# A hybrid attention and state-space kernel: q and k turned once, their parts laid out by DMA, values weighed head by head

## What is computed

```
qkv = x @ qkv_w + qkv_b                      # x: normed, [512, 128]
q, k, v = split(qkv)                         # 16 heads of 8
q, k = rotary(q), rotary(k)
weights = softmax(q k^T * SCALE)             # 512 x 512 per head
x = x + (weights @ v) @ out_w + out_b
```

## Time and profile before

| what | value |
|---|---|
| median of the runs shown | 10320.33 us |
| the profiled execution, its own time | 10330.53 us |
| its span, first to last instruction | 10328.1 us |
| PE, DVE, ACT, POOL busy | 90%, 86%, 70%, 59% |
| mean granted clock of TensorE | 0.986 |
| one sample to the next (load of x to load of x) | 642.4 us |
| attention, first row maximum to the addition at L1371, 16 samples | 72.3 to 75.1 us, mean 73.9 |
| end of L1626 to the next sample's first row maximum, 15 times | 60.5 to 62.3 us, mean 61.4 |

### The profile page before, as it was taken

One profiled execution on the slowest core, in us unless ns is written; L12 is line 12 of the kernel. 1 busy time (PEld: TensorE's weight loads), 2 busy tenths in 40 slices (PEclk: granted clock), 3 DMA queues, 4 the chain that ended last, 5 costly groups with the idle time before them and its releaser, 6 DMA issues.

```text
span 10328.1 us, 259854 instructions
## 1 busy us (share of the span) xinstructions
PE 9306.5 (90%) x88874; PEld 6451.6 (62%) x88874; DVE 8861.6 (86%) x16781; ACT 7278.4 (70%) x15068; POOL 6118.0 (59%) x4900
## 2 busy tenths in 40 slices
PE   7989899898998989989899899999898999899988
PEld 4656656566565665656656566565665656656566
DVE  6978979789797887979879798797987979879798
ACT  5867768677686776857768576685766858668586
POOL 2936829367293772927729277392763928639286
PEclk9999999999999999999999999999999999999999
DMA  0000000000000000000000000000000000000000
GB/s 21 0 3 1 2 3 0 3 1 2 3 0 3 1 2 3 0 3 1 2 3 0 3 1 2 3 0 3 1 2 3 0 3 1 2 3 0 3 1 3
DMA packets 648478, 23.66 MB, mean 2 GB/s; under 512 B 629185, under 2 KB 647250, under 8 KB 647506
## 3 DMA queue, kind: packets, MB, share of 16 engines
q1 hardware_dynamic: 647890, 16.11, 3.7%
HBM read 9.40 MB, written 4.19 MB: 1 GB/s over the span
## 4 chain that ended last, share of the span: by engine, by line
DVE 27%; PE 23%; issue 18%; POOL 17%; ACT 11%; DVEq 1%; POOLq 1%; DMA 0%; SPq 0%; ACTq 0%
POOL work L1700 16%; DVE work L1601 10%; DVE work L1591 6%; ACT scan_in L1099 4%; PE ps L605 4%; PE ps L595 3%; PE ps L590 3%; PE ps L534 2%; PE ps L522 2%; ACT da L983 1%; DVE stats L1223 1%; ACT yscT L1132 1%; DVE scan_in L1505 1%; POOL skip_u L1673 1%; PE ps L801 1%
## 5 line engine op out<-in xcount | busy, mean ns | idle before, releaser
L1700 POOL TENSOR_TENSOR work<-work,crep 128x512 f32<-128x512 f32 x4608 | 5764.0, 1276 | 4134.8 <-DVE work L1540 3631.6
L1099 ACT ACTIVATE scan_in<-du,bcn 128x256 f32<-128x256 f32 x8832 | 3690.6, 498 | 70.5 <-PE ps L811 37.7
L1601 DVE TENSOR_TENSOR_SCAN work<-da,hend,ps 128x256 f32<-128x256 f32 x4608 | 3028.5, 726 | 56.9 <-PE ps L811 47.8
L811 PE MATMUL ps<-w_ident,scan_in 128*128 128x128 f32 x18432 | 2456.3, 278 | 275.9 <-ACT scan_in L1099 147.0
L811 PEld LDWEIGHTS ps<-w_ident,scan_in 128*128 128x128 f32 x18432 | 2019.6, 142 | 873.8 <-DVE work L1601 313.3
L1591 DVE TENSOR_TENSOR_SCAN work<-da,ps 128x512 f32<-128x512 f32 x2048 | 2353.4, 1201 | 38.8
L801 PE MATMUL ps<-work,w_sel 128*32 128x256 f32 x17792 | 1408.6, 390 | 275.4 <-POOL work L1700 274.7
L1017 ACT ACTIVATE work<-ps,w_gate_b 128x512 f32<-128x512 f32 x512 | 351.7, 687 | 870.9 <-PE ps L590 802.8
L801 PEld LDWEIGHTS ps<-work,w_sel 128*32 128x32 f32 x17792 | 376.1, 108 | 755.0 <-POOL work L1700 538.1
L1330 DVE TENSOR_REDUCE smax<-ps 128x1 f32<-128x512 f32 x1024 | 657.7, 685 | 176.4 <-PE ps L499 172.3
L983 ACT ACTIVATE da<-ps 128x512 f32<-128x512 f32 x1024 | 555.8, 605 | 152.3 <-PE ps L522 144.8
(11 more groups left out here) (204 smaller groups left out, 12458.2 us busy)
## 6 DMA issues: line engine op xcount, KB each, us to landing
hend<-work SPq DMA_DIRECT2D x2304, 1.0 KB, 1.8
x_in<-in_x SPq DMA_DIRECT2D x17, 256.0 KB, 2.8
out<-work SPq DMA_DIRECT2D x16, 256.0 KB
gate_w<-in_gate_w SPq DMA_DIRECT2D x1, 1024.0 KB, 5.0
up_w<-in_up_w SPq DMA_DIRECT2D x1, 1024.0 KB, 7.1
down_w<-in_down_w SPq DMA_DIRECT2D x1, 1024.0 KB, 9.1
w_w_zy<-in_w_zy SPq DMA_DIRECT2D x1, 256.0 KB
work<-in_w_mix SPq DMA_DIRECT2D x1, 256.0 KB
```

Source lines behind the costliest of these rows:

```text
L811: mm = eng.transpose(ps[:, bank, c:c + P], scan_in[:, m, tb, 2 * j + s].rearrange("p k c -> p (k c)"), ident[:])
L1099: ins = eng.activation(scan_in[:, m, tb, :, k, :], du[:, hf, tb, :].rearrange("p (e c) -> p e c", c=GC), ACT.Copy, scale=bcn[:, hf, tb, 0, ...
L1601: ins = eng.tensor_tensor_scan(hst[:, p % NHID, half], da[:, 1, 2 * p + s, :], ps[:, RING[p % 4], half], hend[:, 2 * p + s:2 * p + s + 1], ...
L1700: eng.tensor_tensor(prod[:, to, :].rearrange("p (s t) -> p s t", s=2), hst[:, p % NHID, :].rearrange("p (s t) -> p s t", s=2), crep[:, hf, ...
```

## The change

q and k of all heads are turned to feature-major once, by eight fp32 transposes after the rotation (`start`, step 3 on PE). ScalarE and VectorE split the turned array into three parts of [128, 2, 512]. SyncE stores the parts to DRAM (3 DMAs) and loads them from there into the rows of `heads`: 18 DMAs of eight partitions by eight heads by 512, and two for the constant rows, for each half of the heads (`load_heads`). Semaphores `heads_in[0]` and `heads_in[1]` guard heads 0 to 7 and 8 to 15. `turn_head`, `copy_head` and the slot copies are gone.

The norm of the next x moves from the second mixture to the end of the last scan unit, the qkv products to the mixture's beginning. `weigh` takes one head at a time, one key block in each quarter of the array, in two halves of 256 queries at b = 2 and 3 of every iteration; three heads share a bank, and `turn_out` (now a product with a 32-column selector) also sums the four quarters. Rescores rotate through two banks. Every `copy_max` is on ScalarE. There are six outputs to normalise instead of four. Before the loop the preparation of sample 0 runs alone, as before.

```diff
-HG = 4
+HG = 3
+HR = 4
-RESCORE = (3, 4, 6)
+RESCORE = (3, 4)
+QKV_BANK = (6, 2)
-PE_START, ACT_START = (1, 2, 3), (4, 7)
-DVE_START = ((1,), (2,), (3,), (4, 5), (6,), (7,), (8,), (9,))
+PE_ROT = 2
+ACT_START = (9, 11)
+DVE_START = ((5,), (6,), (), (7,), (8,), (0, 2), (), (9,))
+WEIGH_AT = (2, 3)
...
+            def load_heads(at, step=0):
+
+                for n in range(PARTS):
+                    if n < PARTS - 1:
+                        eng.wait_ge(part_a.sem, part_a.count(at, n + 1))
+                    else:
+                        eng.wait_ge(part_v.sem, part_v.count(at, 1))
+                    eng.dma_start(parts_d[n].rearrange("k p t -> p k t"), parts[:, n]
+                                  ).then_inc(parts_kept.sem, parts_kept.up(at))
+                eng.wait_ge(parts_kept.sem, parts_kept.last(at))
+                for g in range(HALVES):
+                    rows = slice(g * HH * HD, (g + 1) * HH * HD)
+                    for k in range(2):
+                        for q in range(SLOTS):
+                            n = q % PARTS if k else q // PARTS
+                            eng.dma_start(
+                                heads[HD * q:HD * (q + 1), g * HH:(g + 1) * HH, k, :],
+                                parts_d[n, k, rows].rearrange("(h c) t -> c h t", c=HD)
+                                ).then_inc(heads_in[g].sem, heads_in[g].up(at))
+                    for k, rows in enumerate((BIAS - QR, BIAS + 2 - QR)):
+                        eng.dma_start(
+                            heads[QR:QR + rows, g * HH:(g + 1) * HH, k, :],
+                            pad_d[k, 0:rows].rearrange("r (o t) -> r o t", o=1).broadcast_to([rows, HH, T])
+                            ).then_inc(heads_in[g].sem, heads_in[g].up(at))
...
                 def score(h, qb):
-                    if qb == 0:
-                        eng.wait_ge(qk_copied.sem, qk_copied.count(at, h + 1))
+                    if qb == 0 and h % HH == 0:
+                        eng.wait_ge(heads_in[h // HH].sem, heads_in[h // HH].count(at, 2 * SLOTS + 2))
...
+                def weigh(h, part):
+
+                    eng.wait_ge(exped.sem, exped.count(at, TB * (h + 1)))
...
+                    q = slice(part * TH, (part + 1) * TH)
+                    for kb in range(TB):
+                        mm = eng.matmul(ps[32 * kb:32 * kb + 32, 7, q],
+                                        vaug[:, kb, h, :], probsT[:, h % HR, kb, q],
+                                        start=(h % HG == 0 and part == 0),
+                                        stop=((h % HG == HG - 1 or h == NH - 1) and part == 1))
...
-                keep_busy(4, 0)
-                turn_head(0)
-                keep_busy(20, 0)
-                turn_head(1)
...
+                weigh(NH - 1, 0)
+                weigh(NH - 1, 1)
+                turn_out(OUTS - 2)
+                turn_out(OUTS - 1)
...
             def mixture(at, coming=None):
-                keep_busy(24, 1)
+                if coming is None:
+                    keep_busy(24, 1)
+                else:
+                    start(coming, 1)
+                    eng.wait_ge(x3_ready.sem, x3_ready.count(at, 1))
+                    start(coming, 2)
+                    keep_busy(4, 1)
...
+                if coming is not None:
+                    eng.wait_ge(qkv_taken.sem, qkv_taken.count(coming, 2))
                 for u in range(4):
                     into(u)
```

More of the change, by code:

```diff
@@ L386, in begin_with @@
             seen = [list(s.seen) for _, s in sems]
-            for step in range(steps):
+            for step in steps:
                 start(Place(0, 0), step)
@@ L530, in weigh @@
                         eng.wait_ge(v_ready.sem, v_ready.count(at, 1))
[L531 to L537 removed]
+                    if h > 0 and h % HG == 0:
+                        eng.wait_ge(o_copied.sem, o_copied.count(at, h // HG))
@@ L627, in mixture @@
                         into(2 * e + 5)
-                    if coming is not None and e in PE_START:
-                        start(coming, PE_START.index(e))
+                    if coming is not None and e == PE_ROT:
+                        eng.wait_ge(summed.sem, summed.count(at, 1))
+                        start(coming, 3)
             def ssm_inputs(at):
@@ L911, in _ @@
             eng.wait_ge(fold_kept, 2)
-            begin_with(start, len(PE_START))
+            begin_with(start, range(4))
             with eng.Fori(0, B) as b:
@@ L1028, in mixture @@
                     if coming is not None and u in ACT_START:
-                        start(coming, ACT_START.index(u))
-                if coming is not None:
-                    for step in range(len(ACT_START), 2 + PARTS):
-                        start(coming, step)
+                        start(coming, 2 + ACT_START.index(u))
             def ssm_inputs(at):
@@ L1184, in _ @@
             eng.wait_ge(prepared, 1)
-            begin_with(start, 2 + PARTS)
+            begin_with(start, range(4))
             with eng.Fori(0, B) as b:
@@ L1206, in _ @@
                 back_v(at, 1, 1)
+                start(Place(b + 1, 0), 1)
                 back_last(at, 1, 1)
@@ L1279, in start @@
                               for n in ("cosine", "sine")]
-                    for half, (first, second, op) in enumerate(((even, odd, ALU.subtract), (odd, even, ALU.add))):
-                        eng.tensor_tensor(ta, first, angles[0], ALU.mult)
-                        eng.tensor_tensor(tc, second, angles[1], ALU.mult
-                            ).then_inc(nchain.sem, nchain.up(at))
+                    first, second, op = ((even, odd, ALU.subtract), (odd, even, ALU.add))[half]
+                    if half == 1:
@@ L1284, in start @@
                         eng.wait_ge(nchain.sem, nchain.last(at))
-                        ins = eng.tensor_tensor(r[:, half], ta, tc, op)
-                        if half == 0:
-                            ins.then_inc(nchain.sem, nchain.up(at))
-                            eng.wait_ge(nchain.sem, nchain.last(at))
-                    ins.then_inc(rot_done.sem, rot_done.up(at))
-                first = [qk_slots[:, :, :, PARTS * n, :] for n in range(PARTS)]
-                full = rot.rearrange("p b (k h c) -> p k b h c", k=2, c=HD)
@@ L1375, in mixture @@
                 norm(at, n_moe, x_res)
+                if coming is not None:
+                    start(coming, 3)
+                    start(coming, 4)
                 eng.wait_ge(routed.sem, routed.count(at, 1))
@@ L1452, in mixture @@
                 eng.wait_ge(vchain.sem, vchain.last(at))
-                if coming is not None:
-                    start(coming, 0)
                 for e in range(NE):
@@ L1646, in _, with begin @@
             eng.wait_ge(prepared, 1)
-            begin_with(start, 10)
+            def begin(at, step):
+                if step < 2:
+                    start_norm(at, step)
+                if step != 1:
+                    start(at, step)
+            begin_with(begin, range(10))
             with eng.Fori(0, B) as b:
```

256 lines of the change are left out of this document (122 added, 134 removed).

## The result

The changed kernel took 10425.12 us (median of 4 runs, 10413.8 to 10432.57) against 10318.11 for the kernel before: ratio 1.0101, interval 1.0089 to 1.0113. Forecast were 10290 and a range up to 10360. Its profiled execution has a span of 10425.1 us, 97.0 more than before. One of the four runs of reads_together, further down, took 25652 us at a granted clock of 0.36 and stands outside its median.

The account below looks back on a forecast made before the run. PE was to pace the attention's heads from the fourth on, the DMA chain its entry; +8.8 - 15 x 1.9 - 16 x 0.2 - 2.5 = -25.4 on 10330.5 gave 10305, by the runs' median 10295, moved to 10290; range 10215 to 10360.

Parts of the forecast that it names:

- Here the DMA chain is late, not VectorE: Second mixture up to heads: stores and loads decide the first maximum, at 59.5 us against 61.4, -1.9 fifteen times.
- I take 13.6: Third part to heads loaded: store 2.8, 20 loads 0.48 apart, the last landing 1.8 to 2.8 later; 13.6 us taken.
- margin of 1.5: Loads of heads: 64 KB takes 0.31 us on eight engines, under the 0.48 issue gap, so the engines keep up.
- heads come late: Rival, loads of heads: bound by packets or latency, each us beyond 15.5 behind the third part costs 15; chance 0.18.
- late case: Loads of heads at 0.8 us each: 21 us, 111 more than forecast, 10400, slower.
- The clock: Attention's beginning at clock 0.50 after some 6 us without PE work: 2.0 us lost, bounds 0 and 4; 0.8 at the end.
- clock stays up: Rival, attention: scores alone keep or raise the clock, 2.8 us an attention back, 45 in all, 10245; chance 0.25.
- Main part, steady state: Attention: PE paces every head from the fourth on at 3.49 us; main part 56.2 us without a cold clock.
- PE's even pace does not hold: Rival, attention: waits for exponentials, split maxima or output turns cost 2.5 us each, 40 in all, 10330; chance 0.12.
- Attention, end: Last maximum to addition: last exponential after 6.7 us, then 8.0 of serial copies, halves, turns and projection; 14.7 together.
- Last mixture: End of the kernel: nobody waits for heads there, so the output is ready 2.5 us earlier.
- The second half is hidden,: Loads of heads 8 to 15: issued by about 24 us behind the third part, wanted 25 us after the first score.

Follow-up runs that it names:

- reads_together: Changed kernel with each load reading, for each of its eight partitions, eight rows that follow one another in DRAM instead of every eighth; 10450.44 us, ratio 1.0134.
- Quarters: Changed kernel with the heads loaded in four quarters instead of two halves (HALVES = 4); 10306.99 us, ratio 0.9984.
- quarters_warm: Changed kernel with heads loaded in four quarters, 40 small transposes ahead of the first score and more behind scores of the first three heads; 10270.95 us.
- warm_between: Changed kernel plus 96 small transposes ahead of the first score, three behind each score of the first two heads, one behind the third's; 10388.95 us.
- image: Changed kernel with heads loaded in four quarters and their nine slots laid out in DRAM by the stores, for fewer, larger loads; 10363.8 us, ratio 1.0038.
- early_parts: Changed kernel with pads first, behind the first part, and six of the first half's loads issued behind each part's store; 10383.82 us, ratio 1.0069.

## Why the prediction was wrong, step by step

*Which step failed.* "Here the DMA chain is late, not VectorE" was right in kind and mis-sized: "I take 13.6", measured 19.1 and the score. The third part was ready at 44.5 (forecast 45.2), the store landed after 2.2 (2.8), and the last load was issued 7.4 behind the first (9.1). What failed is the next term, "and it lands 1.8 to 2.8 later": the last load landed 9.5 us after its issue. The sum took the issue as the pace and the landing as that of a lone DMA, and the loads did not keep up: they formed a backlog.

The check that should have caught it divided a transfer of 1024 KB down to 64 KB, 0.31 us on eight engines, "margin of 1.5". Three things were off in it. 1 KB packets are dearer, 46 ns where few are in flight: 8 x 46 = 0.37 us a load on each of eight engines. SyncE issued a load every 0.38, not 0.48, so the margin was gone. And the two loads of the pads are not of 64 KB but of 192 and 208: with their 16 packets for each engine a half is 176 packets on each of eight engines, 8.1 us at 46 ns. Yet all this explains only a backlog of about a microsecond. The rest is that the packets of 1 KB themselves took 107 ns in the third sample with the backlog standing, for a cause that stays open (below).

5.5 us a sample against the forecast is 5.5 x 15 = 83 us, of which 10 came back because the third part was sooner; the prologue, with the same chain of 23.9, gave 8.3 more. Quarters returns 118 us by one number and so puts the loss there. This is the mechanism of the rival *heads come late*, whose chance of 0.18 was too low; its own point was right too: 19.1 lies 3.6 beyond 15.5, and the entry grew by 2.9.

*The sum.* Against the sum's span (10328.1 - 25.4 = 10302.7) the measured one is 122 longer: 81 for the loads, 29 for the clock, 14 in the stretch between attention and second mixture, less 1 in the last mixture. The range ended at 10360, which the text calls half of the way to the late case; half of the way was 10345, and the result lies beyond the late case itself (10400), with the clock's 29 us on top.

The profile's packets under 512 B rose from 629185 to 635386, by 6201, and in quarters to 640794. By the rule on the number of engines in the Trainium skill (DMA: Bandwidth & Descriptors, Why a DMA increments its semaphore by 16 and not by 1; the prediction names the section before it), with one small packet for each engine at a DMA's end, a data load ends with 8 small packets, a store with 16, the pads' loads of 24 and 26 rows with 12 and 13: 16 x (288 + 48 + 50) plus 25 for the two stores of the pads is 6201. For quarters it gives 11609, and 640794 - 629185 is 11609. The trace agrees: eight engines a load. The forecast had the eight engines, but priced long packets. The 521 packets of 1 KB in the trace of before took 46 ns in the median; 8 x 46 would have cut the margin from 1.5 to 1.3, and would not have said 0.7.

*The clock.* Costed 2.0 at the beginning (bounds 0 and 4) and 0.8 at the end. The main part was 60.0; with fillers between the scores (quarters_warm) 56.16, against 56.2 costed without a cold clock. So the schedule was right to 0.1 us, and the clock cost 3.4 (quarters, 59.58, against quarters_warm) to 3.8, near its bound of 4. What it took beyond the 2.0 costed is 1.8 x 16 = 29 us. Half clock meets the first iterations that weigh: from the fourth head's maxima to the fifth's 5.86 us in the mean, 3.27 with the clock up (warm_between). TensorE's wait ahead of the scores was 12.3 us in the mean of 15 samples, not "some 6". The rival *clock stays up* is out; fillers ahead of the scores alone do not even keep it.

*Main part, steady state.* 3.51 a head (3.49), a turn 0.9 more: right. The lost rescore bank costs nothing, as said. *PE's even pace does not hold* is out.

*Attention, end.* 15.55 against 14.7 + 0.8: right as a total. The last exponentials end 6.75 behind the last maximum (6.7). The terms of the 8.0 behind them add up to 8.1, and no run shows the 0.8 for the clock by itself: in the third sample the clock falls only at 1436.8, in the last 4 us, and with fillers the stretch takes 15.55 to 15.98.

*Last mixture.* 3.9 earlier, 2.5 forecast; VectorE alone would be ready for maxima at 54.0, not 55.5.

*The second half is hidden,* in the changed kernel: yes, no wait for it. But the loads do something else behind it: the engines' code comes later. I had named stores, `hend` and the output as neighbours of the loads, not the code. In the changed kernel this costs little (ScalarE 2.5 us in a wait); in image it decides.

The Trainium skill (Runtime: NRT & Kernel Launch, Instruction fetch mechanics) calls the fetch of the next block of code "mostly hidden". In the kernel before the trace agrees, but for one wait of TensorE of 1.6 to 2.3 us a sample ahead of its small products; image, with 7.0 us of VectorE and 5.2 of TensorE, shows where it does not.

*What stays open.* Why the first half's 64 KB loads go no faster than one per 0.7 us in three unlike ways: with a backlog (99.5 ns a packet), with four in flight (57 ns), and with other patterns (51 and 69 ns, issue-bound). Each has another visible limit, and all give 88 to 105 KB a us. It is no limit of the shape: in the changed kernel the second half, the same shapes to the same partitions, is in 11.1 us after the first in the mean of 15 samples, where the first took 16.9 from its first issue; in the prologue the two took 21.1 and 17.7. The changed kernel's windows (columns as above):

```profile
1358.00:1360.00 2.00, 0.00 (x0) 0.00 (x0) 0.00 (x0) 0.00 (x0) 0.00 (x0) 0.50 0.57 78
1366.00:1368.00 2.00, 2.00 (x5) 0.31 (x3) 2.00 (x4) 0.00 (x0) 0.00 (x0) 0.50 0.66 184
```

The write of the eight neighbouring rows as such is thereby an unlikely cause. What differs between the halves (the rows read in DRAM, the place in the row written, what else is in flight) no run separates, nor the landing time of 2.9 us. Open too is what makes a code block wait. That the engines wait for a block is shown; that the block is late because of the loads rests on image, early_parts and the changed kernel side by side, and no run varies the loads alone.

## What to carry to other kernels

Price a DMA by its packets: packets per engine times the time of a packet of that size, over all loads ahead of the consumer, and compare that with the issue interval. Where the two are near each other count on no cover: a packet took twice as long here once there was a backlog. What counts then is how many bytes stand ahead of the first consumer. Splitting so that it waits for a quarter and not a half returned 118 us, more than the change had lost. Where a change moves work from an engine to DMA, look for what else comes by DMA at that place, the engines' own code above all; and where it empties TensorE, price the clock at the first dense stretch after it, not in the idle one.

## What the runs showed of the hardware

- A 1 KB packet took 52 ns in the mean in quarters (46 in the median), 107 ns in the backlog of the changed kernel's first half. The second half, of the same 1552 KB, landed in 11.1 us where the first took 16.9.
- Two DMAs of the same 64 KB cost SyncE 0.38 or 0.71 us to issue, by nothing but their row pattern; with a full queue the cheap one costs 0.69 too.
- A store of 256 KB landed after 2.2 us alone and behind six loads of 32 KB, after 6.0 behind six loads of 64 KB.
- VectorE stood 6.6 to 7.8 us a sample for its own instructions while loads ran at 178 GB/s; it went on 1.7 to 1.9 us after a block of 8 KB had arrived.
- Two groups of eight fp32 products of 256 columns take 1.00 us back to back and 2 x 0.57 with other shapes between, and one change of shape (0.09) more.
